# Two score banks instead of three, and a fifth bank for the maxima, in the last five stages of an eight-batch transformer kernel

## What is computed

```python
query = split_heads(q @ w_q.T + b_q)        # 16 heads of 16 features, 512 rows
key   = split_heads(k @ w_k.T + b_k)        # 1,601 rows
value = split_heads(v @ w_v.T + b_v)
scores = einsum('bhqd,bhkd->bhqk', query, key) / sqrt(16)
attn = softmax(scores, axis=-1)
x = einsum('bhqk,bhkd->bhqd', attn, value)
```

## Time and profile before

| | us |
|---|---|
| runs | 2868.33, 2864.20, 2868.32 (median 2868.32) |
| the profiled execution | 2870.83 |
| its span, first to last instruction | 2869.1 |
| TensorE busy | 2680.7 (93%) |
| VectorE busy | 1736.8 (61%) |
| ScalarE busy | 1448.1 (50%) |
| mean granted TensorE clock | 0.981 |

### The profile page before, as it was taken

One profiled execution on the slowest core, in us unless ns is written; L12 is line 12 of the kernel. 1 busy time (PEld: TensorE's weight loads), 2 busy tenths in 40 slices (PEclk: granted clock), 3 DMA queues, 4 the chain that ended last, 5 costly groups with the idle time before them and its releaser, 6 DMA issues.

```text
span 2869.1 us, 39579 instructions
## 1 busy us (share of the span) xinstructions
PE 2680.7 (93%) x13707; PEld 1292.3 (45%) x13707; DVE 1736.8 (61%) x4231; ACT 1448.1 (50%) x2923; POOL 281.4 (10%) x344
## 2 busy tenths in 40 slices
PE   7878999999999999999999999999999979989998
PEld 3533433353334433443444333433344323349998
DVE  3346676667766776577666766677666767751111
ACT  2232565546564565457555655465545656733332
POOL 1200100011000100020002000100001000002222
PEclk8998999999999999999999999999999989989999
DMA  5431322323132413240424123231323022039995
GB/s 181 122 101 47 91 51 66 102 64 85 41 109 64 112 41 107 53 117 18 119 49 112 46 75 94 70 85 35 108 60 86 18 63 67 18 123 370 375 376 209
DMA packets 215142, 296.37 MB, mean 103 GB/s; under 512 B 50534, under 2 KB 180814, under 8 KB 214935
## 3 DMA queue, kind: packets, MB, share of 16 engines
q1 hardware_dynamic: 198428, 221.50, 27.6%
q0 software_dynamic: 16512, 72.32, 7.3%
HBM read 232.87 MB, written 60.50 MB: 102 GB/s over the span
## 4 chain that ended last, share of the span: by engine, by line
PE 79%; DVE 9%; ACT 5%; issue 5%; DMA 1%; SPq 0%; POOL 0%; ACTq 0%; POOLq 0%; DVEq 0%
PE PS L1500 12%; PE PS L1452 11%; PE PS L1483 10%; DVE mxC L2022 7%; PE PS L1135 6%; PE PS L1110 6%; PE PS L1682 5%; PE PS L1694 5%; PE PS L1164 3%; PE PS L1337 3%; PE PS L1231 2%; PE PS L1254 2%; PE PS L1123 2%; ACT reg L1001 2%; ACT reg L888 2%
## 5 line engine op out<-in xcount | busy, mean ns | idle before, releaser
L1001 ACT ACTIVATE reg<-PS 128x512 f32<-128x512 f32 (+1 forms) x1664 | 962.0, 598 | 935.4 <-PE PS L1483 929.7
L2022 DVE TENSOR_REDUCE mxC<-PS 128x1 f32<-128x400 f32 (+1 forms) x2048 | 1096.4, 570 | 554.1 <-PE PS L1452 541.3
L1452 PE MATMUL PS<-reg 96*128 96x400 bf16 (+1 forms) x2048 | 672.0, 340 | 70.2 <-DVE mxC L2022 38.3
L1483 PE MATMUL PS<-reg 99*128 99x512 bf16 (+1 forms) x1664 | 609.3, 385 | 22.4 <-ACT reg L1001 17.5
L1452 PEld LDWEIGHTS PS<-reg 96*128 96x128 bf16 x2048 | 196.5, 98 | 588.4 <-DVE mxC L2022 437.8
L1500 PE MATMUL PS<-reg 128*17 128x512 f32 (+1 forms) x3328 | 441.4, 602 | 1.1 <-ACT reg L1001 0.5
L1483 PEld LDWEIGHTS PS<-reg 99*128 99x128 bf16 (+1 forms) x1664 | 163.7, 100 | 347.1 <-ACT reg L1001 186.9
L1135 PE MATMUL PS<-reg 128*128 128x512 f32 (+1 forms) x416 | 211.6, 601 | 0.5 <-ACT reg L875 0.5
L1110 PE MATMUL PS<-reg 128*128 128x512 f32 (+1 forms) x512 | 209.3, 523 | 1.1 <-ACT reg L902 0.7
L1047 ACT ACTIVATE reg<-PS,reg 128x128 f32<-128x128 f32 x312 | 89.0, 368 | 217.6 <-issue 113.3
L1682 PEld LDWEIGHTS PS<-reg 128*128 128x128 f32 x1248 | 147.8, 194 | 3.1 <-issue 1.0
(11 more groups left out here) (233 smaller groups left out, 2558.4 us busy)
## 6 DMA issues: line engine op xcount, KB each, us to landing
reg<-in_D_W SPq DMA_DIRECT2D x78, 1024.0 KB
reg<-in_A_mask POOLq DMA_DIRECT2D x32, 800.5 KB, 6.2
dramK<-reg SPq DMA_DIRECT2D x144, 100.0 KB
dramV<-reg SPq DMA_DIRECT2D x48, 272.0 KB, 3.1
reg<-in_ctxT POOLq DMA_DIRECT2D x8, 1601.0 KB, 10.3
reg<-in_ctx POOLq DMA_DIRECT2D x8, 1536.0 KB, 7.7
dramQ<-reg SPq DMA_DIRECT2D x96, 128.0 KB
reg<-dramQ SPq DMA_DIRECT2D x32, 384.0 KB, 6.8
```

The costliest lines, as they stand in the source:

```text
L1001: act.activation(pr[u % RING][0:r, :], PS[0:r, S_PLAN[NU * b + u][0], :], ACT.Exp).then_inc(a_expC, 1)
L1452: last = mm(PS[:, bank, 0:w], qs[(NG * bb + g) % 3][0:ROWS, h, t * P:(t + 1) * P], ks[g % 2][0:ROWS, h, c0:c0 + w], start=True, stop=True)
L1483: last = mm(PS[0:r, bank, :], ks[g % 2][0:STK, h, c * P:c * P + r], qs[(NG * b + g) % 3][0:STK, h, :], start=True, stop=not with_mask)
L2022: v.tensor_reduce(mxC[:, h, t, j:j + 1], PS[:, M_PLAN[bb, g, i][0], 0:M_CH[j][1]], AX.X, ALU.max).then_inc(v_mx, 1)
```

## The change

The same instructions stand in the same order on every engine. What changes is in which bank a tile goes, and so what it waits for:

| stage | score banks | maxima banks (made in this stage) |
|---|---|---|
| (6,3) | 5, 6, 3 -> 5, 6 | 0, 1, 2 -> 0, 1, 2, 3 |
| (7,0) | 5, 6, 3 -> 5, 6 | 0, 1, 2 -> 0, 1, 2, 3 |
| (7,1), (7,2) | 5, 6, 3 -> 5, 6 | 0, 1, 2, 4 -> 0, 1, 2, 3, 4 |
| (7,3) | six banks, as before | none |

One TensorE wait goes, that of the first score tile of (6,3) for the last projection's read of bank 3; the first maxima tile of the stage, two steps on, had and has the same wait.

```diff
 MB, F0, F1, F2, SB, VB = (0, 1), 2, 3, 4, (5, 6), 7
-MB_END = MB + (F0, F2)
+MB_END = MB + (F0, F1, F2)
...
     if bb < B - 1:
         return MB
-    return MB_END[:3] if g < 2 else MB_END
+    return MB_END[:4] if g < 2 else MB_END
...
         ring = SB
         if U >= NU * B - UN:
             ring = SB + (F1,) + MB + (F0,)
-        elif U >= NU * (B - 1) - UN:
-            ring = SB + (F1,)
         bank = min(ring, key=lambda k: last.get(k, -1))
...
                 past(pe, a_expC, before)
-                if U == NU * (B - 1) - UN:
-                    pe.wait_ge(v_tq, 2 * B)
                 if U == NU * B - UN:
                     pe.wait_ge(v_mx, NG * NSC * B)
```

## The result

The changed kernel takes 2872.61 us (median of 14 runs) where the kernel before takes 2865.52 (median of 14). The ratio is 1.0024 with a 95% interval of 1.0014 to 1.0034: slower by 7.1 us, and 0.24% is clear of the interval. The forecast was 2875.8 us from a median of 2868.3, that is +7.5.

The account below looks back on a forecast made before the run. TensorE was taken as the bound, with VectorE level in (7,1). Terms +0.9, -0.7, +3.7, +3.7 and 0 made +7.6, taken as +7.5 on 2868.32: 2875.8 us, range 2867 to 2881 (own range 2872 to 2880).

Parts of the forecast that it names:

- (6,3), from step 8 on: Stage (6,3): maxima gain and score stall nearly cancel, nine cycles from 3.24 to 3.28 us plus border +0.48; +0.9 us.
- (7,0), gain of the fourth maxima bank: Stage (7,0): waits for VectorE's reductions go, 3.5 us at most, taken as 3.0 us saved.
- (7,0), stalls of the scores: Stage (7,0): step 2 +0.63, step 50 +0.48, and 0.29 us in some four places, +1.2.
- The distance rule: All score tiles with two banks: none can start sooner than 1.07 us after the tile two before it.
- Nine cycles of 0.29: Regular steps 10 to 42 of a stage: one 0.29 us stall per four steps, 2.99 to 3.28 us, nine times.
- The lower bound: If the two-bank wait cost nothing: (6,3) gains 10 x 0.25 us and (7,0) 3.0, total -5.5 us.
- TensorE as the only full engine: (7,1): TensorE's issue times fill the 2.99 us of four steps, so nothing takes a stall back.
- rival 2: (7,1), (7,2): stall mostly taken back, only borders cost, 2 x 1.1 us; +2.4, 2870.7 us; chance 0.22.
- Rival 1: Regular steps: two-bank wait hidden, only the maxima banks' gain left; -5.5 us, 2862.8 us; chance 0.07.
- Rival 3: Regular stalls drop TensorE's clock to 1.2 GHz, some 30 us more per stage, 2906 us or over; chance 0.03.
- Hidden in the load: Step 2 of (6,3): score stall costs nothing, since TensorE waits 11.99 us right behind it for a query load.
- Hidden before the transposes: Step 46 of (6,3), (7,0), (7,2): 0.4 us stall covered by the transposes' 1.41 us wait for VectorE.

Follow-up runs that it names:

- e1: Against the change: two score banks kept, maxima back on the rings of the kernel before, bank 3 idle until (7,3); 1.0031 of before, 2874.81 us.
- r2: The kernel before, unchanged, run once more for a second profile; one run, 2865.47 us.
- e2: Against the change: no fifth maxima bank, maxima made in (7,1) and (7,2) keep four banks (0,1,2,4); 1.0029 of before.
- e7: Against the change: maxima tiles of the regular steps laid 2,1,2,1 instead of 1,1,2,2, same banks; 1.0001 of before, 2866.69 us.
- e3: Against the change: maxima tiles of the regular steps laid 2,2,2,0 instead of 1,1,2,2, same tiles and banks; 0.9996 of before, 2863.70 us.
- r1: The changed kernel, unchanged, run once more for a second profile; one run, 2874.80 us.
- e4: Against the change: new banks in (6,3) and (7,0) only, rings of before from (7,1) on; 0.9993 of before.
- e6: Against before: bank 4 for maxima in (6,3); in (7,0) bank 3 serves maxima in steps 3 to 47, scores at both borders; 2857.23 us, 0.9970.
- e5: Against the kernel before: idle bank 4 serves as fourth maxima bank in (6,3), scores keep three banks; 0.9995 of before.

## Why the prediction was right

Right, with each term near its size. Taken from stages without a stretch at half clock, and for (6,3) from the steps behind it:

| term | forecast | measured |
|---|---|---|
| (6,3), from step 8 on | +0.9 | +1.0 (36.5 against 35.6, in both profiles of each) |
| (7,0), gain of the fourth maxima bank | -3.0 | -3.1 (e1 54.3, the change 51.2) |
| (7,0), stalls of the scores | +2.3 | +2.1 (e1 54.3, r2 52.2) |
| (7,1) | +3.7 | +3.6 (e1 43.5 against 39.8) |
| (7,2) | +3.7 | +3.6 (e1 43.2 against 39.6) |
| (7,3) | 0 | 0 (25.7 us from its first to its last score tile in all profiles) |
| sum | +7.5 | +7.2; by the medians +7.1, by the interval +4 to +10 |

- **The distance rule** came from one row in which a third tile waited in the batches before, and held to 0.02 us: 1.07 in the change, in e1 and e2, 1.08 in e7, and 1.09 at the borders. It was the right row since it gave a distance between starts, which carries over; its wait of 0.47 us would not have.
- **Nine cycles of 0.29** were 2.6 us in the sum and 2.5 measured: the first of the nine took 3.16 us before, not 2.99, and so lost 0.13; the other eight lost 0.30 each. (The lower bound counts ten cycles in (6,3); there are nine.)
- **TensorE as the only full engine** in (7,1): the sum of its issue times was the cycle, and so nothing took the stall back. VectorE looked as full, which was rival 2's ground; e2 shows that a bank more or less for it changes nothing there.
- **Rival 1** (the stall is hidden) fell in (7,1) and (7,2). What it needed, 1.07 us of work between the tiles, is there in e3.
- **Rival 3** (the clock) is not what moved the time: e1 has the same stalls and 3.6 us a stage with the clock at 1.00 throughout (7,1) and (7,2). But it isn't refuted as an addition. Behind the 1.6 us wait for the transposes of (7,1) the clock fell for 6.8 us in the change and in e2, and for 13.7 in r1, not in e1, e3 and e7; for 3.4 us in r2, e4 and e6, and not in before and e5. The longest ones are with two score banks and 1,1,2,2, but e1 has both and none. Nine kernels with one or two profiles each don't settle it. The rest of the program differs too: behind the last score tile both profiles of the change take 336.3 us, with 17 us at half clock, and those of before 339.8 and 338.6, with 26 and 23. Whether this belongs to the stretches ahead of it is not shown.
- **Hidden in the load** (step 2 of (6,3)) is neither shown nor refuted. From the first score tile to the first maxima tile it was 12.8 and 13.8 us in the two profiles of before, and 13.6 and 13.5 in the two of the change: the load varies by more than the 0.63 us that are asked about.
- **Hidden before the transposes** (step 46) held. The stall is there: in (7,2) the score tile of step 46 starts 1.07 us behind the tile two before it in place of 0.61. But steps 44 to 47 take 4.03 us before and after, since the transposes' wait for VectorE fell from 1.4 to 0.9 us. (6,3) and (7,0) show the same.
- **Missed**, and without effect on the sum: how far single executions differ. The first profiles of the two kernels differed by 3.4 us in (6,2), where nothing was changed: before had 10 us at half clock there, the change none.

The rules of the Trainium skill that the prediction weighed: use of all eight PSUM banks ("Perfetto Trace Analysis", section "Matmul Optimizations") does not tell the two kernels apart from (7,1) on, where both use all eight and are 3.6 us a stage apart. In (6,3) bank 4 idles in both, and there the runs agree with it: putting it to use took 2.2 us off (e5). The clock swing of a kernel that cycles through PSUM banks ("TensorE: Matmul & The Clock Gate", section "A second HAM failure mode: psum-queue depth-cycling") did not come with the short stalls in e1: it has 0.29 us of them in every 3.29 us, and its granted clock is 1.00 over (7,1) and (7,2).

## What to carry to other kernels

A ring of n banks is a distance: tile k may start one producer-consumer round trip after tile k - n. Read the round trip off one row where such a wait is seen, lay it against the starts of the tiles, and look at the closest run of them, not at the mean. Where it falls short, the order of the work between the tiles can do what a bank does, for nothing (the regular steps of e3), if the other stream's ring is deep enough for its new runs (e3 and e7 in (6,3)). A bank moved from one stream to another should follow the runs of both: give it to a stream in the steps where that has its run, and back (e6).

## What the runs showed of the hardware

- From the start of a 128x512 score matmul to the start of its exponential it is 0.42 us, and from there to the next matmul in the same bank 0.65: 1.07 us for a round trip whose busy parts are 0.38 and 0.60.
- Consecutive exponentials start 0.49 to 0.5 us apart where rows of one last 0.60, and reductions of 400 columns 0.49 to 0.50 apart where one lasts 0.57: a row's length overstates what the next one waits.
- Stretches at 1.2 GHz have other places or other lengths in each execution of one kernel. One of 3.4 us on a group's border costs 1.2 us (r2: 41.0 in place of 39.8), a sixth of the whole effect studied here; one inside (7,0) costs 1.6 (53.8 in place of 52.2).
- Single executions differ most ahead of the stages studied: the first score tile of (6,3) starts at 2304.3 us in one profile and at 2313.4 in another, after the same instructions. Lengths of stages, counted by the starts of one kind of tile, repeat to 0.02 us where the clock is the same (51.17 and 51.18 in (7,0) of the change, 39.61 in (7,2) of before, e5 and e6), and show effects of 2 us that whole times hardly do.
